# The position terms of a bias network move from GpSimd to VectorE

## What is computed

```python
pos = grid_q[:, :, None, :] - grid_kv[:, None, :, :]
bias = jnp.sign(pos) * jnp.log1p(jnp.abs(pos))
bias = jax.nn.relu(bias @ cpb_w1 + cpb_b1)      # 2 -> 128
bias = jax.nn.relu(bias @ cpb_w2 + cpb_b2)      # 128 -> 128
bias = (bias @ cpb_w3 + cpb_b3).reshape(b, GROUPS, H * W, Hd * Wd)
```

## Time and profile before

| what | value |
|---|---|
| time, median of 3 executions | 4365.64 us (4363.87 to 4365.74) |
| time of the profiled execution | 4366.62 us |
| its span, first to last instruction | 4364.8 us |
| mean granted clock of TensorE over the span | 0.944 |
| loop of the change, 64 iterations of | 33.3 us each |

### The profile page before, as it was taken

The page is one execution under the profiler, slowest core; times in us unless marked ns, Lnnn a source line. Parts: engine busy times, 40 slices in busy tenths (PEclk is TensorE's granted clock), DMA queues, the critical chain, the costliest instruction groups (busy, mean ns, idle before and its releaser), DMA issues. The chain is left out here.

```text
span 4364.8 us, 67125 instructions
## 1 busy us (share of the span) xinstructions
PE 3896.5 (89%) x18472; PEld 2384.1 (55%) x18472; DVE 2992.5 (69%) x4467; ACT 2579.8 (59%) x4583; POOL 2118.7 (49%) x1861
## 2 busy tenths in 40 slices
PE   2699999999999999999998999788888377969999
PEld 1455555555555555555556777547666242435553
DVE  7788888888888888888886333447888833235562
ACT  3599999999999999999994333222121330113331
POOL 1555555555555555555551555306667500026663
PEclk7799999999999999999999999889999677989999
DMA  1200000000000000000002000219999911353311
GB/s 45 98 9 11 10 9 9 11 10 9 11 9 9 9 11 10 9 10 10 10 9 81 0 0 0 69 51 350 371 387 376 341 46 60 137 140 69 69 40 77
DMA packets 146902, 326.59 MB, mean 75 GB/s; under 512 B 45737, under 2 KB 46761, under 8 KB 145789
## 3 DMA queue, kind: packets, MB, share of 16 engines
q1 hardware_dynamic: 105340, 174.46, 12.9%
q0 software_dynamic: 41472, 151.01, 8.9%
HBM read 246.14 MB, written 79.04 MB: 74 GB/s over the span
## 5 line engine op out<-in xcount | busy, mean ns | idle before, releaser
L502 POOL TENSOR_TENSOR cpb_sum<-cpb_tab 128x512 f32<-128x512 f32 x1028 | 1045.9, 1048 | 965.7 <-DVE cpb_r L632 965.4
L613 ACT ACTIVATE cpb_h<-cpb_z,net_vec 128x512 f32<-128x512 f32 x1536 | 1006.1, 697 | 50.7 <-PE cpb_z L553 38.2
L550 PE MATMUL cpb_z<-cpb_r,cpb_w2a 128*128 128x512 f32 x2048 | 858.6, 419 | 23.5 <-DVE cpb_h L673 23.5
L632 DVE SCALAR_TENSOR_TENSOR cpb_r<-cpb_sum,cpb_r 128x512 fp32r<-128x512 f32 x1024 | 695.4, 710 | 187.8 <-ACT cpb_r L607 187.8
L551 PE MATMUL cpb_z<-cpb_r,cpb_w2b 128*128 128x512 f32 x2048 | 801.3, 391 | 0.0
L553 PE MATMUL cpb_z<-cpb_r,cpb_w2a 128*128 128x512 f32 x2048 | 799.8, 391 | 0.0
L632 DVE SCALAR_TENSOR_TENSOR cpb_r<-cpb_z,cpb_r 128x512 fp32r<-128x512 f32 x1028 | 661.8, 685 | 160.3 <-ACT cpb_r L607 154.6
L607 ACT ACTIVATE cpb_r<-cpb_z 128x512 fp32r<-128x512 f32 x1028 | 560.4, 604 | 139.5 <-PE cpb_z L537 139.5
L607 ACT ACTIVATE cpb_r<-cpb_sum 128x512 fp32r<-128x512 f32 x1024 | 598.5, 648 | 2.0 <-POOL cpb_sum L502 2.0
L550 PEld LDWEIGHTS cpb_z<-cpb_r,cpb_w2a 128*128 128x128 f32 x2048 | 384.0, 187 | 365.9 <-issue 301.0
L1480 DVE SCALAR_TENSOR_TENSOR dc_acc<-dc_g,dc_wt,dc_acc 128x512 f32<-128x512 f32 x560 | 444.3, 799 | 57.8 <-DMA dc_g<-conv_out,dc_idx 42.0
(11 more groups left out here) (336 smaller groups left out, 5243.2 us busy)
## 6 DMA issues: line engine op xcount, KB each, us to landing
conv_out<-dc_ys SPq DMA_DIRECT2D x576, 64.0 KB, 6.5
cpb_log<-log_dram SPq DMA_DIRECT2D x66, 256.0 KB, 3.1
qk_parts<-gn_r SPq DMA_DIRECT2D x64, 256.0 KB, 2.0
dc_wr<-in_dc_wT SPq DMA_DIRECT2D x9, 1024.0 KB, 5.9
bias_dram<-cpb_bst SPq DMA_DIRECT2D x520, 8.0 KB
net_x<-in_x SPq DMA_DIRECT2D x8, 1024.0 KB, 10.1
sa_qa<-qk_parts SPq DMA_DIRECT2D x16, 512.0 KB
sa_ka<-qk_parts SPq DMA_DIRECT2D x16, 512.0 KB
```

The costliest lines, as they stand in the source:

```text
L502: pool.tensor_tensor(SUM[:, r, :].rearrange("p (y x) -> p y x", x=W), TAB[:, slot, r, 0, :].unsqueeze(1).broadcast_to([P, NF // W, W]), TA ...
L550: pe.matmul(z2[:, bank, :], W2A[:], R1[:, k, :], start=True, stop=False)
L613: act.activation(H2[:, t % 8, :], z2[:, t % 3, :], ACT.Relu, bias=V("cpb_b2")).then_inc(h2a, 1)
L632: v.scalar_tensor_tensor(R2[:, t % RING, :], first_layer(t), 0.0, R1[:, t % RING, :].bitcast(F32), ALU.max, ALU.subtract).then_inc(r2_read ...
```

## The change

GpSimd no longer makes `EXP` for the following iteration. VectorE makes it, half 0 in its step t = 16 and half 1 in its step t = 24, directly after the two table instructions and ahead of the low part of tile 23 or 31. The waits that keep `EXP` from being overwritten too early (`z1_ready`) ask for the same counts as before. The two spreads ahead of the loop stay on GpSimd. `spread` itself is the same function.

```diff
@@ -512,18 +512,13 @@
             with pool.Fori(0, ITERS) as i:
-                nxt = (i + 1) % ITERS
 
                 pool.wait_ge(r2_ready, i * TPI + 8)
                 sums(3, i * 2 + 1)
-                pool.wait_ge(z1_ready, i * 4 + 2)
-                spread(pool, bass.ds(nxt, 1), 0)
                 pool.wait_ge(r2_ready, i * TPI + 16)
                 sums(5, i * 2 + 2)
                 pool.wait_ge(r2_ready, i * TPI + 24)
                 sums(7, i * 2 + 2)
-                pool.wait_ge(z1_ready, i * 4 + 4)
-                spread(pool, bass.ds(nxt, 1), 1)
                 pool.wait_ge(r2_ready, i * TPI + 32)
                 sums(9, i * 2 + 3)
@@ -667,6 +662,9 @@
                             v.wait_ge(sum_ready, i * (TPI // 2) + (t // 8 - 1) * 8)
                             v.wait_ge(log_in, i * 16 + 32)
                             table(t // 8 - 2)
+
+                            v.wait_ge(z1_ready, i * 4 + t // 4 - 2)
+                            spread(v, bass.ds((i + 1) % ITERS, 1), t // 8 - 2)
                         second_part(i, t + 4 + k)
```

## The result

The changed kernel takes 4405.0 us (median of 6), against 4363.87 us for the kernel before on the same chip: ratio 1.0094, 95% interval 1.0081 to 1.0107, slower by 41 us. The forecast was 4396 us, slower by 31 us against the 4365.64 us known then.

The account below looks back on a forecast made before the run. TensorE sets the pace and waits only for VectorE's read-out. Stalls of 0.47 + 0.03 us, taken as 0.48, over 64 iterations add 31 us to 4366.6, giving 4397, or 4396 as median; forecast band 4386 to 4406, range 4377 to 4418.

Parts of the forecast that it names:

- GpSimd's part, gain 0: Two 1.04 us adds per iteration leave GpSimd; nobody waits for them and the contention removed was hidden, so nothing is gained.
- S = 0.60: VectorE's time for one spread, in us, estimated from a 691 ns fp32 tensor_tensor whose successor starts before its end.
- The register work: Sequencer work for the spread's wait and address, claimed hidden behind low part 22 and the tables: 0, at most 0.15 us per spread.
- The upper bound: Longest cost of a spread on VectorE, from the longest low part beside GpSimd, 1027 ns: 0.94 us.
- First stall, 0.47: Step 16: tile 18's late read-out stalls TensorE at tile 21 by 0.37 us, plus 0.10 for an uncovered weight load.
- Second stall, 0.48, of which 0.45 absorbed: Step 24: read-out 26 comes late, TensorE stalls at tile 29; its existing wait at tile 0 absorbs all but 0.03 us.
- the old stall: Turn of the iteration, kernel before: TensorE starts tile 0 0.45 us late, waiting for VectorE's read-out of tile 30.
- Sum, 0.50, taken as 0.48: Both spreads' net cost per iteration, 0.47 + 0.03 us, lowered to 0.48; over 64 iterations 31 us slower.
- The cheap spread: Rival: VectorE adds bf16 at double rate, a spread costs 0.33 us, 13 us slower, 4379 us; chance 0.12.
- Both are paid: Rival: both spreads count, or register work shows: 4416 us, or 4427 if nothing is absorbed; chance 0.16.
- The collision that I called hidden: GpSimd's spread stretched VectorE's low-part pair from 1.29 to 1.62 us; the 0.33 us was claimed covered by ScalarE idle time.
- What would show it: Trace signs: two VectorE spreads, iteration 33.78 us, TensorE waits about 0.35 us at tiles 21 and 29, nearly none at tile 0.

Follow-up runs that it names:

- read-outs 18 and 26 early: The change, with VectorE's read-outs of tiles 18 and 26 moved ahead of the tables and spread in steps 16 and 24: 4365.98 us, before 4366.64.
- the fixed address: The change, but both spreads read key group 0 at the same address in every iteration: 4405.01 us, before 4366.47.
- both behind the read-out: The change, with both VectorE spreads placed after the read-outs of steps 16 and 24 instead of ahead of the last low part: 4393.04 us, before 4364.37.
- the exchange: The kernel before, with VectorE's read-out of tile 30 moved ahead of the low part of tile 35 in step 28: 4338.07 us, before 4366.47.
- The doubled spread: The change, with a second spread into a spare buffer ahead of each spread: 4478.97 us, before 4366.47.

## Why the prediction was right, and where its size was off

- *GpSimd's part, gain 0.* Right. Its waits grew by about what its work lost and the span gained, and the low parts on `SUM` fell from 695.4 to 672.7 us in the page's sums. The kernel with read-outs 18 and 26 early has the same work off GpSimd, and its time is that of before. One reading was wrong without effect: the pair that I took as undisturbed has one input in PSUM and ran beside GpSimd's sums. A pair on `SUM` away from GpSimd takes 1.29 us too.
- *S = 0.60.* 0.60 to 0.61 by the starts (row of 0.685). The register work is hidden: the fixed address changed the loop by under 2 us. The upper bound was no bound: a meeting with GpSimd stretched a spread to 1.24 us in the kernel with both behind the read-out, and a low part to 1.31 us with the first spread only and to 1.44 with read-outs 18 and 26 early, instead of 1.03. How long it gets depends on how early in GpSimd's instruction VectorE's starts.
- *First stall, 0.47.* 0.49 at tile 21, and 0.50 per iteration when it stands alone. Off by 0.03.
- *Second stall, 0.48, of which 0.45 absorbed.* The stall was 0.49 and the old stall 0.44, by the distance from tile 31 to tile 0 in the change itself, in the second spread alone and with the exchange. Both terms are right to 0.01. The 0.99 us of the last layer, for which the prediction showed no row, is the 2031.07 to 2032.06 above. Alone, the second spread cost 0.05 to 0.07 per iteration instead of 0.03.
- *Sum, 0.50, taken as 0.48.* The steps gave 0.50 and I rounded it down for no reason in the rows. Measured 36.6 / 64 = 0.57 over the whole loop, and 33.89 - 33.30 = 0.59 without the first iteration. No term is badly off, but all the misses point the same way: 0.02 of rounding, 0.02 to 0.03 in the first stall, 0.01 each in the second and in the reserve, and 0.03 to 0.05 in small delays of the tiles behind a stall, 0.01 us or less each, which the sum put at nothing. What makes those isn't shown.
- *The size.* The loop grew by 37 us instead of 31; the span of the profiled execution grew by 38.6 and the median by 41.1. The interval of the measurement is 35 to 47 us, so 31 lies outside it: the forecast of the difference was too small. The time of 4405.0 us is inside the forecast's 4386 to 4406 by 1 us only, and with some luck, since the kernel before took 1.8 us less beside it than the 4365.64 that I had added to.
- *Rivals.* The cheap spread is refuted for these operands and confirmed as a price. "Both are paid" sets in a little below S = 0.60, not at it: by the measured terms the second stall reaches the reserve when S - 0.22 + 0.11 = 0.44, at S = 0.55 (an estimate). The doubled spread shows that beyond it both count. The collision that I called hidden in the kernel before, and used only as a gain that does not count, decided two experiments.
- *What would show it.* Two spreads on VectorE, two waits, none at tile 0, GpSimd at 16.3 us: all seen. The iteration is 33.89 us, not 33.78. The waits show as 0.20 to 0.23 us, not 0.35, because a bracket counts from the modelled end of the last matmul; the distances of the starts show the full stall.

## What to carry to other kernels

In a loop of engines with orders written by hand, price an added instruction by what stands behind it on its queue and by when that is needed, not by the engine's load: the same 0.61 us cost 0.50, 0.05 to 0.07 or nothing per iteration here. A stall that another engine already has once per loop is a reserve that absorbs a later delay of that engine, so a cheap-looking addition may be spending what a simple exchange would have gained (28 us here). When moving work between VectorE and GpSimd, look at what the other one reads at that moment too.

## What the runs showed of the hardware that was not expected

A VectorE instruction with two SBUF inputs that started while a GpSimd add of this loop was running finished only after it. There are 892 such meetings in eight of the traces (64 to 128 in each), and in all of them VectorE's instruction ended 0.54 to 0.55 us after GpSimd's add. So a spread of 0.685 us took 1.09 to 1.25 us, and a low part of 0.69 us took 0.72 to 1.44, the longer the earlier in GpSimd's add it started. With both spreads behind the read-out, the add that was running took 1.05 us, as alone; the one behind it took 1.50 us in all 128 meetings and ended 0.91 us after the spread. Low parts with one input in PSUM took 0.67 to 0.70 us beside the same adds, in all traces. The rows show the times; that each side waits for the other's running instruction is the plainest reading of them.

From the end of VectorE's read-out to the start of the matmul that waits for it there are 0.13 to 0.14 us in the rows shown of three kernels.
